# Ternary feed-forward weights prepared inside cross-attention instead of at the head of the feed-forward stage

## The reference

```
x = x + attention(layernorm(x))                     # linear attention, gated, Wq Wk Wv Wo, G1 G2
x = x + cross_attention(layernorm(x), context)      # softmax, 16 heads of 32, w_q, w_kv, w_proj, relative bias
x = x + ffn(layernorm(x))

def weight_quant(w):                                # ternary
    scale = 1 / clip(mean(|w|), 1e-5)
    return clip(round(w * scale), -1, 1) / scale
def act_quant(x):                                   # 8 bits, per row
    scale = 127 / clip(max(|x|), 1e-5)
    return clip(round(x * scale), -128, 127) / scale
ffn(x) = bitlinear(silu(bitlinear(x, w_gate)) * bitlinear(x, w_up), w_down)
```

## Time and profile before

| | |
|---|---|
| median of 3 runs | 1415.78 us (1412.97 to 1416.22) |
| profiled execution | 1415.03 us |
| its span, first to last instruction | 1413.10 us |
| mean granted clock of TensorE | 0.953 |
| busy: TensorE, VectorE, ScalarE, GpSimd | 1242.2, 861.0, 561.8, 165.7 us |
| self-attention | to about 323 us |
| cross-attention | from 327.6 to about 1172 us |
| feed-forward | from 1173.8 us to the end |

### The profile page before, as it was taken

One profiled execution on the slowest core, in us unless ns is written; L12 is line 12 of the kernel. 1 busy time (PEld: TensorE's weight loads), 2 busy tenths in 40 slices (PEclk: granted clock), 3 DMA queues, 4 the chain that ended last, 5 costly groups with the idle time before them and its releaser, 6 DMA issues. The chain is left out here.

```text
span 1413.1 us, 27116 instructions
## 1 busy us (share of the span) xinstructions
PE 1242.2 (88%) x10602; PEld 956.2 (68%) x10602; DVE 861.0 (61%) x1555; ACT 561.8 (40%) x923; POOL 165.7 (12%) x246
## 2 busy tenths in 40 slices
PE   4799999980599999999999999999999873689997
PEld 3688888860577787787887878777878653344443
DVE  5766666642456656566566666565655535688884
ACT  2222222220324334334343433343343334477775
POOL 0011111123000101010101111011101011011110
PEclk9999999995699999999999999999999995899999
DMA  5222222225443244253243242432432208212111
GB/s 155 85 72 87 88 88 85 71 71 129 109 119 76 71 110 109 51 135 83 69 117 94 74 121 61 125 97 62 115 85 67 71 23 295 105 53 67 59 62 42
DMA packets 69002, 129.23 MB, mean 91 GB/s; under 512 B 12644, under 2 KB 24996, under 8 KB 68396
## 3 DMA queue, kind: packets, MB, share of 16 engines
q1 hardware_dynamic: 65740, 116.90, 29.7%
q0 software_dynamic: 3168, 11.01, 2.3%
HBM read 68.71 MB, written 11.07 MB: 56 GB/s over the span
## 5 line engine op out<-in xcount | busy, mean ns | idle before, releaser
L1122 DVE TENSOR_REDUCE xa_m_part<-xa_psM 112x1 f32<-112x376 f32 x512 | 265.4, 546 | 227.1 <-PE xa_psM L1293 223.2
L1041 ACT ACTIVATE xa_space<-xa_psS 125x448 f32<-125x448 f32 x384 | 207.5, 545 | 251.0 <-PE xa_psS L1277 247.8
L1293 PE MATMUL xa_psM<-xa_k,xa_q 104*112 104x376 f32 x512 | 155.7, 349 | 8.1 <-DVE xa_m_part L1122 6.3
L1277 PE MATMUL xa_psS<-xa_q,xa_k 104*125 104x224 f32 x768 | 144.4, 271 | 0.5 <-ACT xa_space L1041 0.5
L1277 PEld LDWEIGHTS xa_psS<-xa_q,xa_k 104*125 104x125 f32 x768 | 136.6, 187 | 7.4 <-issue 1.1
L1317 PE MATMUL xa_psO<-xa_space,xa_cv 125*32 125x224 f32 x1536 | 110.6, 360 | 1.3 <-ACT xa_space L1041 1.3
L1317 PE MATMUL xa_psO<-xa_space,xa_ones 125*32 125x224 f32 x1536 | 108.2, 354 | 0.0
L1293 PEld LDWEIGHTS xa_psM<-xa_k,xa_q 104*112 104x112 f32 x512 | 88.5, 175 | 26.4 <-DVE xa_m_part L1122 11.1
L1263 PE MATMUL xa_psR<-xa_cT_hi,xa_w_hi 128*128 128x376 f32 x256 | 88.8, 347 | 14.6 <-DVE xa_cT_lo L1112 7.7
L1263 PE MATMUL xa_psR<-xa_cT_hi,xa_w_lo 128*128 128x376 f32 x256 | 90.5, 354 | 0.0
L1263 PE MATMUL xa_psR<-xa_cT_lo,xa_w_hi 128*128 128x376 f32 x256 | 87.6, 342 | 0.0
(11 more groups left out here) (198 smaller groups left out, 2578.9 us busy)
## 6 DMA issues: line engine op xcount, KB each, us to landing
xa_k<-xa_k_st SPq DMA_DIRECT2D x384, 94.0 KB, 2.2
xa_cv<-in_ctx_dram SPq DMA_DIRECT2D x8, 1500.0 KB
xa_q<-xa_q_st SPq DMA_DIRECT2D x192, 56.0 KB, 2.0
sa_fw<-in_L_ffn_w_gate_dram SPq DMA_DIRECT2D x8, 512.0 KB, 4.6
sa_fw<-in_L_ffn_w_up_dram SPq DMA_DIRECT2D x8, 512.0 KB, 6.0
sa_fw<-in_L_ffn_w_down_dram SPq DMA_DIRECT2D x8, 512.0 KB, 7.4
ff_w_raw<-in_L_ffn_w_gate_dram SPq DMA_DIRECT2D x4, 1024.0 KB, 9.2
ff_w_raw<-in_L_ffn_w_up_dram SPq DMA_DIRECT2D x4, 1024.0 KB, 14.1
```

The costliest lines, as they stand in the source:

```text
L1041: nc.scalar.activation(pT[:, (s + i) % 2, j], psS[0:KB, (HG * i + j) % NB, 0:2 * N], ACT.Exp).then_inc(exp_done, 1)
L1122: V.tensor_reduce(m_part[:, seg, t, jj:jj + 1], psM[0:T, seg, 0:SEG], AX.X, ALU.max, negate=True).then_inc(mx_read, 1)
L1277: last = M.matmul(psS[0:KB, (HG * i + j) % NB, a * N:(a + 1) * N], k4[0:ROWS, s % 2, j, col:col + KB], q4[0:ROWS, s, j, :], start=True, st ...
L1293: M.matmul(psM[0:T, seg, 0:SEG], q4[0:ROWS, g, jj, t * T:(t + 1) * T], k4[0:ROWS, g % 2, jj, seg * SEG:(seg + 1) * SEG], start=True, stop= ...
```

## The change

The preparation of the weights moves out of ternary_ffn and into cross_attention, in 24 units of 128 x 1024 (8 for each weight), one for each step of batches 0 to 5. A step gets a 17th beat. For a unit: SP loads 512 KB into f_raw, ScalarE rounds it in place after beat 9, GpSimd makes it ternary in bf16 (f_tern), TensorE turns it as a filler "W" in beat 15 or 16 through a psR bank, VectorE copies it with the maximum into f_out (which shares f_raw's memory), and SP stores 256 KB to DRAM. There is one such buffer, so the load of a unit waits for the store of the one before it. SP does store and load in next_ffn, placed behind the packing of keys of each step; unit 0 is loaded ahead of the loop. In the last batch, behind load_residual, SP loads the turned weights from DRAM over the query, key and value weights in w_hi and w_lo. The scales are computed at the head of cross_attention. ternary_ffn takes the weights where they lie and has no preparation left.

```diff
...
-    BEATS = 16
+    BEATS = 17
     halves_at = [range(0, 1), range(1, 2), range(2, 4), range(4, 5), range(5, 7), range(7, 8), range(8, 10),
-                 range(10, 11), range(11, 13), range(13, 14), range(14, 16)] + [range(0)] * 5
+                 range(10, 11), range(11, 13), range(13, 14), range(14, 16)] + [range(0)] * 6
     unit_at = [(k // HG, k % HG) if k < UNITS else None for k in range(BEATS)]
     attend_at = {5: 0, 9: 1, 13: 2}
     TURN_AT = 12
-    parts_of = {"V": 3, "K": 3, "Y": 3, "q": 1, "r": 1, "X": 1}
+    I = ffn_weights[0].shape[0]
+    WC = 2 * D
+    TURNS = I * D // P // WC
+    UNITS_W = 3 * TURNS
+    ROUND_AT = 9
...
+        {0: "K2a", 3: "K2b", 6: "Xa", 7: "Xb", 8: "Y0", 11: "q2", 12: "q3", 13: "Y1", 16: "W"},
+        {0: "K3a", 3: "K3b", 6: "r0", 7: "r1", 8: "q0", 9: "r2", 10: "r3", 11: "q1", 12: "r4", 13: "r5", 15: "W"},
+        {0: "K0a", 3: "K0b", 6: "V0", 9: "V1", 12: "V2", 15: "W"},
+        {0: "K1a", 3: "K1b", 6: "V3", 9: "V4", 12: "V5", 15: "W"},
...
+        f_raw = sb("f_raw", [P, WC])
+        f_out = f_raw[:, 0:WC // 2].bitcast(BF16)
+        f_tern = space[:, 2 * HG * 2 * N:2 * HG * 2 * N + WC // 2].bitcast(BF16)
...
+            def load_ffn(unit):
+                n, t = divmod(unit, TURNS)
+                if unit >= 1:
+                    sp.wait_ge(f_stored, DMA * unit)
+                w = ffn_weights[n].rearrange("(a p) k -> p a k", p=P)
+                src = w[:, 2 * t:2 * t + 2] if n < 2 else w[:, :, 2 * t * P:2 * (t + 1) * P]
+                sp.dma_start(f_raw[:].rearrange("p (a k) -> p a k", a=src.shape[1]), src).then_inc(f_in, DMA)
+            def store_ffn(unit):
+                n, t = divmod(unit, TURNS)
+                sp.wait_ge(f_out_ready, unit + 1)
+                if n < 2:
+                    dst = gu_dram[n][:, :, 2 * t * P:2 * (t + 1) * P]
+                else:
+                    dst = down_dram[:, 2 * t:2 * t + 2]
+                sp.dma_start(dst, f_out.rearrange("p (k c) -> p k c", k=dst.shape[1])).then_inc(f_stored, DMA)
+            def next_ffn(b, s):
+                unit = NG * b + s - 1
+                if 0 <= unit < UNITS_W:
+                    store_ffn(unit)
+                    if unit + 1 < UNITS_W:
+                        load_ffn(unit + 1)
+            def load_turned():
+                for n, w in enumerate((w_hi, w_lo)):
+                    half = slice(n * I // P // 2, (n + 1) * I // P // 2)
+                    sp.dma_start(w[:, 2].rearrange("p k n -> p (k n)").bitcast(BF16),
+                                 down_dram[:, half].rearrange("p a d -> p (a d)")).then_inc(ffn_loaded, DMA)
+                for n, w in enumerate((w_hi, w_lo)):
+                    sp.dma_start(w[:, 0:2].rearrange("p a k n -> p (a k n)").bitcast(BF16),
+                                 gu_dram[n].rearrange("p k i -> p (k i)")).then_inc(ffn_loaded, DMA)
...
+            load_ffn(0)
             for b in range(B):
                 if b >= 1 and b + 1 < B:
                     load_context(b + 1)
                 pack_keys(b, 2)
+                next_ffn(b, 0)
                 if b + 2 < B:
                     load_x(b + 2)
                 pack_keys(b, 3)
+                next_ffn(b, 1)
                 load_residual(b)
                 if b + 1 < B:
                     pack_queries(b + 1, 0)
                     pack_keys(b + 1, 0)
+                    next_ffn(b, 2)
                     pack_keys(b + 1, 1)
+                    next_ffn(b, 3)
                     pack_queries(b + 1, 1)
+            sp.wait_ge(f_stored, DMA * UNITS_W)
+            load_turned()
+            sp.wait_ge(ffn_loaded, 4 * DMA)
...
+            def ternary(unit):
+                pool.wait_ge(f_rounded, unit + 1)
+                if unit >= 1:
+                    pool.wait_ge(f_out_ready, unit)
+                nc.gpsimd.tensor_scalar(f_tern, f_raw[:], MAGIC, 1.0, ALU.subtract, ALU.min).then_inc(f_tern_ready, 1)
+                pool.wait_ge(f_tern_ready, unit + 1)
             rstd(0)
             rstd(1)
             for b in range(B):
                 for s in range(NG):
+                    if NG * b + s < UNITS_W:
+                        ternary(NG * b + s)
...
+            def round_weight(unit):
+                n = unit // TURNS
+                act.wait_ge(f_in, DMA * (unit + 1))
+                act.wait_ge(w_scale_step, 3)
+                nc.scalar.activation(f_raw[:], f_raw[:], ACT.Identity, bias=magic[:], scale=w_inv[:, n:n + 1]).then_inc(f_rounded, 1)
             def exponentials(b, s, i, j):
                 n = NG * b + s
                 if j == 0 and NB * n + i >= 2:
@@ -1060,6 +1155,8 @@
                             take(*ended)
                         if unit := unit_at[k]:
                             exponentials(b, s, *unit)
+                        if k == ROUND_AT and NG * b + s < UNITS_W:
+                            round_weight(NG * b + s)
...
+                if what[0] == "W":
+                    dve.wait_ge(full[r], use_of[what, b])
+                    V.tensor_scalar(f_out, src.bitcast(BF16), -1.0, None, ALU.max).then_inc(f_out_ready, 1)
+                    dve.wait_ge(f_out_ready, b + 1)
+                    dve.sem_inc(read[r], 1)
...
+            dve.wait_ge(w_totalled, 1)
+            V.tensor_scalar(w_mean[:], psR[:, 0, 0:3], 1.0 / (I * D), TINY, ALU.mult, ALU.max).then_inc(w_scale_step, 1)
+            dve.wait_ge(w_scale_step, 1)
+            V.reciprocal(w_inv[:], w_mean[:]).then_inc(w_scale_step, 1)
+            V.tensor_scalar(w_deq, w_mean[:], 1.0 / QMAX, None, ALU.mult).then_inc(w_scale_step, 1)
...
+                elif what[0] == "W":
+                    n, t = divmod(b, TURNS)
+                    pe.wait_ge(f_tern_ready, b + 1)
+                    wide = out.bitcast(BF16)
+                    for m in range(WC // P):
+                        if n < 2:
+                            k, a = divmod(m, 2)
+                            cols = a * D + k * P
+                        else:
+                            k, a = divmod(m, KT)
+                            cols = a * 2 * P + k * P
+                        last = M.transpose(wide[:, m * P:(m + 1) * P], f_tern[:, cols:cols + P], ident_b[:])
+                    last.then_inc(full[r], 1)
+                    return
...
+            M.matmul(psR[:, 0, 0:3], ones[:], w_abs, start=True, stop=True).then_inc(w_totalled, 1)
+            pe.wait_ge(w_scale_step, 1)
+            pe.wait_ge(consts_f, 2)
...
+        gu_T = [w[:, 0:2].rearrange("p a k n -> p (a k n)").bitcast(BF16).rearrange("p (k i) -> p k i", k=KT) for w in (w_hi, w_lo)]
+        down_T = [w[:, 2].rearrange("p k n -> p (k n)").bitcast(BF16).rearrange("p (k d) -> p k d", d=D) for w in (w_hi, w_lo)]
...
             load_x(0)
-            for n in range(3):
-                if n == 1:
-                    load_x(1)
-                for p in range(PARTS):
-                    a = w_dram(n, p).shape[1]
-                    sp.dma_start(w_part(n, p)[0].rearrange("p (a k) -> p a k", a=a), w_dram(n, p)).then_inc(w_in[n][p], DMA)
+            load_x(1)
...
-            round_weight(0)
-            round_weight(1)
...
-            weight_scales()
             statistics(0)
             normalise(0)
             round_x(0)
-            finish_weight(0)
+            dequantisers(0)
             statistics(1)
-            finish_weight(1)
-            dve.wait_ge(w_scale_step, 3)
-            dequantisers(0)
             hidden(0, 0)
             normalise(1)
             hidden(0, 1)
             round_x(1)
-            finish_weight(2)
...
-            M.matmul(psY[:, 0:3], ones[:], w_abs, start=True, stop=True).then_inc(w_totalled, 1)
-            turn_weight(0)
-            turn_weight(1)
             turn_x(0)
-            pe.wait_ge(w_T_ready, 2 * TURNS)
             for c in range(NC):
                 gate_up(0, c)
             turn_x(1)
-            turn_weight(2)
-            pe.wait_ge(w_T_ready, 3 * TURNS)
...
```

More of the change, by code:

```diff
@@ L755, in fillers @@
     def fillers(b, s):
-        return {k: (what, batch_of(what, b)) for k, what in fill[s].items() if 0 <= batch_of(what, b) < B}
+        found = {}
+        for k, what in fill[s].items():
+            if what == "W":
+                if NG * b + s < UNITS_W:
+                    found[k] = what, NG * b + s
+            elif 0 <= batch_of(what, b) < B:
+                found[k] = what, batch_of(what, b)
+        return found
     def part_at(b, s, k):
@@ L950, in _ @@
             pool.wait_ge(const_made, 5)
+            nc.gpsimd.memset(magic[:], MAGIC).then_inc(consts_f, 1)
+            nc.gpsimd.affine_select(out=ident_b[:], in_=ones[:], compare_op=ALU.is_equal, fill=0.0, base=0,
+                                    pattern=[[1, P]], channel_multiplier=-1).then_inc(consts_f, 1)
+            pool.wait_ge(consts_f, 2)
             nc.gpsimd.memset(k4[ROW_SHIFT:ROW_SHIFT + HG].bitcast(F32), 0.0).then_inc(const_made, 1)
@@ L1011, in take @@
```

(38 more changed lines are left out.)

81 lines of the change are left out of this document (17 added, 64 removed), and 4 rows, old and new, of the table fill.

## The result

The changed kernel takes **1697.26 us** (median of 4 runs, 1696.27 to 1698.64), the kernel before in the same comparison 1414.38 (1409.16 to 1416.22, 4 runs): ratio 1.2008, 95% interval 1.1986 to 1.2031. The forecast was 1717, the range 1640 to 1800. The profiled execution of the changed kernel has a span of 1694.7 us, that of before 1413.1: +281.6.

The account below looks back on a forecast made before the run. TensorE was taken to bound cross-attention (97.4 of 100 us busy). Stalls 254, clock 39, weight beat 43, batches 6 and 7 1, start 2, feed-forward -37 gave +302 us on 1415.03: 1717 us, range 1640 to 1800.

Parts of the forecast that it names:

- The order on SyncE: SyncE's queue in cross-attention: weight load issued only after the same step's key packing, so 23 of 24 steps stall.
- The price of a stall: Packing's end to the held attend: store, load, rounding, two exponentials, 9.95 us; 254 us over 23 stalls, ends 200 and 310.
- The clock: TensorE behind each stall: some 3.4 us at 1.2 GHz, costing 1.7 us each, 39 in all, ends 18 and 58.
- The weight beat: End of each of 24 steps: transposes 0.5 and late divide 1.3, 1.8 us per step, 43 in all, ends 12 and 60.
- The late divide: VectorE at step end: copy or Y1's take ahead of the divide delays the next maxima; 1.3 us per step.
- GpSimd: Ternary operation on 1024 columns after rounding: 3.5 us at most, covered by about 5 us, costs nothing.
- rival (c): Weight beat: stalls exist but GpSimd is later, 8 us for 1024 columns, 3 us more per step, 1789 us; chance 0.10.
- Rival (a): ScalarE after beat 9: data already there, VectorE's backlog hides behind fillers; -23 us, 1392 us; chance 0.03.
- rival (b): SyncE's queue: load issued ahead of packing's last waits, TensorE loses 1 to 3 us per step; 1470 us; chance 0.03.
- Rival (d): Cross-attention: stall there, but terms at their short ends; 1605 to 1640 us; chance 0.09.
- named as a sign: In the changed kernel's profile: ScalarE idle 13 to 15 us ahead of rounding, released by the weight load, 23 times.
- The ends: Cross-attention's start 2 us later, ends 0 and 4; final loads hidden; feed-forward 37 us shorter, ends 33 and 40.

Follow-up runs that it names:

- e1: Changed kernel with next_ffn's store and load moved ahead of the packing (of keys; in one step, of queries): 1457.48 us, ratio 1.0305 to the kernel before.
- e8: e1 with the store and load of step 0 also ahead of the context load: 1430.14 us, ratio 1.0124 to the kernel before.
- e9: Changed kernel with the turned unit written over the ternary unit's place, so the next load doesn't wait for the store: 1425.75 us, ratio 1.0090 to the kernel before.
- e12: Changed kernel with 140, 150 and 160 dummy matmuls ahead of the last attend in stalled steps 0, 2 and 3, none in step 1: 1676.13 us.
- e11: Changed kernel with 140, 150 and 160 dummy matmuls ahead of the last attend in steps 0, 2, 3 and 215 ahead of q1 in step 1: 1745.40 us.
- e10: e9 with weights turned in the seventeenth beat of every step and the divide ahead of the last take: 1406.72 us, ratio 0.9949 to the kernel before.
- e7: e1 with weights turned in the seventeenth beat, divide ahead of the last take, and store and load ahead of the context load: 1418.57 us, ratio 1.0044.
- e3: Changed kernel with 130 dummy matmuls ahead of the last attend of every stalled step: 1720.08 us, ratio 1.2173 to the kernel before.

## Why the prediction was right

**The order on SyncE.** Right, as argued: 23 stalls, none for unit 0, behind the packing of the same step. e1, e8 and e9 change only orders and places and take away 240 to 271 us.

**The price of a stall**, by its own steps. The store cost 2.64 us with its wake-up (taken: 2.9 and 0.1), the load 3.43 in the stall shown and 3.9 on average over the 23 (taken: 4.6 and 0.1), rounding and two exponentials 2.15 (taken: 2.25). From packing's end to attend it was 8.27 and not 9.95. Attend or q1 stood 8.10, 12.52, 8.78 and 9.92 us in steps 0 to 3 of batch 3 (forecast 9.8, 12.9, 10.5, 10.8). On their two lines TensorE's waits come to 230.8 us, 221 more than in e9 and 218 more than in the kernel before; the forecast was 254. The mis-sized step is the load, read from a row where other loads follow it closely.

The Trainium skill (DMA: Bandwidth & Descriptors, the fit in section Anatomy of one DMA — SWDGE (gpsimd) path) makes the load 3.2 and the store 2.6. It states the fit for transfers issued by GpSimd; SyncE issues these. The trace agrees with it on the stores to the gate and up places (2.6), shows 2.3 for those of w_down, and lies between page and forecast on the load. The total by the page's figures, 1678, and mine, 1717, are both some 20 us off.

The landings in the page of the changed kernel (KB each, median us from issue to landing):

```profile
xa_f_raw<-in_L_ffn_w_gate_dram SPq DMA_DIRECT2D x8, 512.0 KB, 3.7
xa_gu<-xa_f_raw SPq DMA_DIRECT2D x16, 256.0 KB, 2.6
xa_f_raw<-in_L_ffn_w_down_dram SPq DMA_DIRECT2D x8, 512.0 KB, 3.9
xa_down<-xa_f_raw SPq DMA_DIRECT2D x8, 256.0 KB, 2.3
```

**The clock.** Forecast 1.7 per stall, 39 in all. The traces give more: 34 us in the 17 stalls of steps 0, 2 and 3 (e12 and e9) and 11 in the six of step 1 (e11 and e9), 45 in all or 2.0 per stall. The term was too small by 6. The slow stretch was read rightly from the one gap in the kernel before (3.4 us there, 3.5 here), and half of it fits steps 1 and 2 (1.8 and 1.7 on average). Steps 0 and 3 lose 2.3 and 2.0, for a reason that stays open.

**The weight beat.** Forecast 43 for the 24 steps and 1 for batches 6 and 7; e9 has 43.0 and 4.1, taken from one last attend to the next. The split was off. In e10, with VectorE's divide in front, 20 of the 24 distances are 0.6 to 0.9 us longer than before; it is taken for TensorE's own part (forecast 0.5), which no run tests by itself. The late divide (taken: 1.3 in every step) costs nothing between the last attends of steps 1 and 2 and about 1.5 us in most others. Of the 18.6 us that e10 wins over e9 in the loop, 4.1 are won in batches 6 and 7, where only Y1's take stood ahead of the divide; 1 was forecast for it.

**GpSimd** took 3.64 us for its 1024 columns, 0.14 above what I had called the most, and cost nothing: rival (c) needed 8. Rival (a), the outcome on the other side, failed on the order of the queue; e10 has that outcome, the data there at beat 9, at 1407 instead of 1392: some 12 us of the difference are the four steps with late keys, 4 the weight beat of 0.7 and not 0.5 per step. In rival (b) SyncE gets ahead of the packing's last waits; the queue shows none of that. Rival (d) would have needed 1640 or less; the waits came out 33 us short of their forecast, the other costs came out above theirs. ScalarE's idle time ahead of a rounding was 12.8 us on average, a little under the 13 to 15 named as a sign.

**The ends.** Start +4.0 (forecast 2, end 4), feed-forward 39.7 shorter (forecast 37, end 40); the final 6 MB are issued from 1450.45 on and the last lands 18.4 us after its issue, well ahead of 1495.12.

**The sum.** The loop is longer than before by 317.3 us: 47.1 are the weight beat (e9), 221 the waits, 45 the clock. That leaves 4 us without a place, 1.4 of them behind the last attend of step 1. With +4.0 at the start and -39.7 in the feed-forward this is the 281.6 of the span. The forecast had +302. It is right in its mechanism and in each term's rank; that it came within 20 us is in part luck, since waits too dear by 33 us were set against a clock too cheap by 6, the 4 without a place and a weight beat, a start and a feed-forward off by 2 or 3 each.

## What to carry to other kernels

When a load is issued from an in-order queue, find the last wait ahead of it on that queue, and compare its time in the trace with the first use. Here the queue came free 6.5 us after ScalarE asked for the data (723.24 against 716.73), store, load and rounding came on top, and three engines stood 23 times. If a buffer forces store, then load, then use in a row, another place for the result can take the whole chain off the path at no memory (e9), before anything is tuned inside it. And put added work for VectorE behind what the next step waits for: with the copy and Y1's take behind the divide instead of ahead of it the loop was 18.6 us shorter (e9 to e10).

## What the runs showed of the hardware

- A store of 256 KB issued 0.5 us behind a load of 1.5 MB on the same queue held up the next wait for 14.8 us instead of 2.6, and its issue lasted 5.07 us instead of 0.59 (e1). Twelve packing DMAs of 94 KB, the first issued 3.7 us behind such a load, took 10.6 us to issue instead of some 8.4, and TensorE waited 13.7 us for packed keys in five batches (e7).
- TensorE came back at half clock after 3.08 us without work (e3) and at full clock after 2.06 us (e12), both after some 8 us of small matmuls.
- Behind a stall of 8 to 13 us TensorE worked some 3.5 us at half clock in the stretches shown, and that cost 2.0 us per stall on the critical path (34 us for 17 stalls, e12 against the changed kernel; 1.8 us in each of six, e11).
